# The second sample of attention is loaded during the last tile of the projections, into the projections' own weights buffer

## The reference

```python
q = einsum('bsd,ed->bse', x, Wq)         # 32 heads of 128
k = einsum('bsd,ed->bse', x, Wk); v = ...(Wv)    # 8 heads of 128
q, k = rope(rmsnorm(q)), rope(rmsnorm(k))
kc = k_cache[block_table].reshape(b, 512, 8, 128); vc = v_cache[block_table]...
scores = einsum('bqhd,bkhd->bhqk', q, [kc, k]) * SCALE, masked by cache_seqlens
o = einsum('bhqk,bkhd->bqhd', softmax(scores), [vc, v])
x = x + einsum('bse,de->bsd', o, Wo)
```

## Time and profile before

| | |
|---|---|
| median of 3 runs | 2142.75 us (2140.83 to 2142.89) |
| profiled execution, device time | 2139.18 us |
| span of its trace | 2137.4 us |
| PE busy | 96% of the span |
| granted TensorE clock, mean | 0.99 |
| last matmul of the projections' blocks | starts at 740.4 us |
| first matmul of attention | 753.3 us |

### The profile page before, as it was taken

How to read it: one execution, slowest core, us unless ns; L and a number is a source line. 1 busy time by engine, 2 the same in 40 slices (tenths; PEclk the granted TensorE clock), 3 DMA queues, 4 the chain that set the end, 5 groups by cost and what they waited for, 6 DMA issues and landing times.

```text
span 2137.4 us, 55695 instructions
## 1 busy us (share of the span) xinstructions
PE 2060.5 (96%) x17217; PEld 1346.7 (63%) x17217; DVE 1673.6 (78%) x4284; ACT 1476.5 (69%) x4204; POOL 1102.1 (52%) x1854
## 2 busy tenths in 40 slices
PE   5898999999999878999999999999999999999999
PEld 3444555555555456777777777777777777777775
DVE  7787888887877676778777777777777777777774
ACT  2575777777777766777777777777777777777774
POOL 4464656565666544545445454545454545454542
PEclk9999999999999989999999999999999999999999
DMA  9555787876677589988888888788888888887881
GB/s 352 188 204 168 220 255 225 249 221 210 205 235 246 195 296 280 302 262 250 248 257 249 248 250 259 240 253 249 250 250 248 254 254 246 251 256 246 250 243 55
DMA packets 415961, 513.97 MB, mean 240 GB/s; under 512 B 67251, under 2 KB 313907, under 8 KB 413108
## 3 DMA queue, kind: packets, MB, share of 16 engines
q1 hardware_dynamic: 378292, 375.65, 57.3%
q0 software_dynamic: 37376, 134.76, 19.6%
HBM read 413.77 MB, written 92.54 MB: 237 GB/s over the span
## 4 chain that ended last, share of the span: by engine, by line
PE 60%; SPq 1%; DVE 1%; DMA 1%; issue 1%; ACT 0%; POOL 0%; POOLq 0%; DVEq 0%; ACTq 0%
PE att_scores L1619 15%; PE att_y L1669 15%; PE att_tr L1628 11%; PE att_o L1655 5%; PE att_o L1656 5%; PE att_o L1657 5%; PE att_tr_new L1634 1%; PE att_o L1658 1%; PE att_scores L1620 1%; SPq L126 1%; SPq L120 1%; DMA att_keys<-k_parts 1%; DVE att_prob L1772 0%; DMA att_values<-v_parts,att_idx 0%; DVE att_tpl L1796 0%
## 5 line engine op out<-in xcount | busy, mean ns | idle before, releaser
L1772 DVE CUSTOM_DVE_ANT_0 att_prob<-att_scores,att_mask 128x544 f32<-128x544 f32 x512 | 370.7, 724 | 291.6 <-PE att_scores L1620 238.5
L1698 ACT ACTIVATE att_tph<-att_tr 128x512 f16<-128x512 f32 x512 | 305.9, 597 | 326.2 <-PE att_tr L1628 316.4
L1568 POOL CAST att_parts<-att_norm 128x96 f16<-128x96 f32 x512 | 135.1, 264 | 560.9 <-issue 553.5
L1669 PE MATMUL att_y<-att_wo,att_ot 128*128 128x512 f16 x1536 | 407.6, 379 | 0.0
L1796 DVE TENSOR_TENSOR att_tpl<-att_tr,att_tph 128x512 f16<-128x512 f32 x512 | 349.9, 683 | 0.6 <-ACT att_tph L1698 0.5
L1628 PE MATMUL att_tr<-ident,att_norm 128*128 128x128 f32 x2048 | 325.8, 282 | 0.0
L1225 POOL TENSOR_TENSOR proj_rn<-proj_ra,proj_rb 128x512 f32<-128x512 f32 x128 | 190.3, 1487 | 204.0 <-DVE proj_rb L1334 191.7
L1655 PE MATMUL att_o<-att_tph,att_values 128*128 128x128 f16 x1536 | 284.0, 219 | 2.7 <-ACT att_of L1698 2.3
L1657 PE MATMUL att_o<-att_tph,att_values 128*128 128x128 f16 x1536 | 284.0, 219 | 0.0
L1656 PE MATMUL att_o<-att_tpl,att_values 128*128 128x128 f16 x1536 | 283.9, 219 | 0.0
L1789 DVE TENSOR_SCALAR att_norm<-att_prob,att_col 128x544 f32<-128x544 f32 x512 | 254.2, 497 | 1.0 <-issue 1.0
(11 more groups left out here) (227 smaller groups left out, 5301.6 us busy)
## 6 DMA issues: line engine op xcount, KB each, us to landing
room<-k_parts SPq DMA_DIRECT2D x512, 128.0 KB, 2.7
att_keys<-k_parts SPq DMA_DIRECT2D x512, 128.0 KB
q_parts<-proj_turned SPq DMA_DIRECT2D x128, 256.0 KB, 3.6
v_new_parts<-proj_vp SPq DMA_DIRECT2D x64, 256.0 KB, 3.1
room<-q_parts SPq DMA_DIRECT2D x32, 512.0 KB, 6.8
att_query<-q_parts SPq DMA_DIRECT2D x32, 512.0 KB
w<-in_w_t SPq DMA_DIRECT2D x12, 1024.0 KB, 21.5
room<-in_k_t SPq DMA_DIRECT2D x8, 1024.0 KB, 5.9
```

The lines of the kernel that those rows point to most:

```text
L1669: last = mm(y_ps[:, :], ot[p][:, a, h, :], wo[:, h, w, :], start=(h == 0 and start), stop=(h == HQ - 1 and stop))
L1698: copy = lambda out, in_, **kw: nc.scalar.activation(out, in_, ACT.Copy, **kw)
L1772: v.tensor_tensor_reduce(out=prob[q][:, :], in0=sc[q], in1=mask[bi % 2][:, at:at + LK], scale=1.0, scalar=-3.0e38, op0=ALU.add, op1=ALU.ma ...
```

## The change

`w` becomes a buffer of the whole program and is laid out by chunk first, `[P, WN, KD, 2, WC]`. Its first half (chunks 0 to 2) is used by blocks 0 to 5 alone. When the last tile has made these, the second sample's keys, query, all four parts of its values and its fresh values are loaded there, and the two parts of the first sample's values that were fetched at the start of attention. SP issues the 26 transfers at step 7 of the last tile, POOL its 6 gathers after its sums 6 to 9. In attention sample 1 is not loaded again, 24 of the 32 heads of `wo` lie in the second half of `w`, and its 8 pieces are issued in another order. The weights' loads in mixing keep their number and size, but write two runs of 4 KB in each partition where they wrote one of 8 KB.

```diff
+SAMPLE = 16 * (NPP + 2 + HB + BT)
...
+        w = keep("w", [P, WN, KD, 2, WC], F16)
...
+        half = WN // 2 * KD * 2 * WC
+        columns = w[:, :, :, :, :].rearrange("p c k h m -> p (c k h m)")
+        take = taker(columns[:, 0:half], half)
+        keys1 = take([NPP + 1, HK, 2, PS], F16)
+        query1 = take([HK, 2, P], F16)
+        values1 = [take([HK, 2, HD], F16) for _ in range(LC)]
+        fresh1 = take([HK, HD], BF16)
+        values0 += [take([HK, 2, HD], F16) for _ in range(LC - EV)]
+        wo_here = columns[:, half:2 * half].rearrange("p (h two d) -> p h two d", two=2, d=D)
...
-            w = mid("w", [P, KD, WN, 2, WC], F16)
...
-                sp.dma_start(raw(i), w_t[k * P:(k + 1) * P, c:c + CH]).then_inc(w_in[i // 3], 16)
+                sp.dma_start(raw(i), w_t[k * P:(k + 1) * P, c:c + CH].rearrange("p (n m) -> p n m", m=WC)).then_inc(w_in[i // 3], 16)
...
+        LATER = {6: (2,), 7: (3, 4), 8: (5, 6), 9: (7,)}
...
+            def second_sample():
+
+                sp.wait_ge(early, SAMPLE)
+                sp.wait_ge(blk_done, (NT - 1) * BLK + BLK // 2)
+                load_sample(nc, sp, 1, 0, 1, keys[1], query[1], rscale[1], page0, k_d, kn_d, q_d, rs_d, early)
+                load_fresh(sp, 1, fresh[1], vn_d, early)
...
+                    if t == NT - 1 and n == BLK // 2 + 1:
+                        second_sample()
...
-            sp.wait_ge(early, 16 * (NPP + 2 + HB + BT))
...
+            def later_values(c):
+
+                if c == EV:
+                    pool.wait_ge(early_values, 16 * EV)
+                    pool.wait_ge(blk_done, (NT - 1) * BLK + BLK // 2)
+                g.indirect_dma_start(out=values[c // LC][c % LC][:, :, :].rearrange("p h two d -> p (h two d)"),
...
                     add(t, n)
+                    if t == NT - 1 and n >= BLK // 2:
+                        for c in LATER[n]:
+                            later_values(c)
...
-        WO_BEHIND = {1: (0,), 2: (1, 2), 3: (3,), 4: (4,), 5: (5,), 6: (6,), 7: (7,)}
+        WO_BEHIND = {0: (0, 1, 2), 2: (3, 4), 3: (5,), 4: (6,), 5: (7,)}
...
-                    if past or bi:
+                    if past or bi > 1:
                         load(t, bi)
...
-                    if c >= 0 and (bi < BT or not (isinstance(t, int) and t == NT - 1)):
+                    if c >= 0 and (bi < BT or t < NT - 1) and t * BT + bi > 1:
                         gather(t * BT + bi, bi % 2, c)
```

More of the change, by code:

```diff
@@ L198, in conditional_residual @@
         fresh0 = take([HK, HD], BF16)
-        page0 = take([NPP], I32)[0:1]
-        first = (keys0, query0, values0, fresh0, rscale0, page0)
+        page0 = take([2 * NPP], I32)[0:1]
+        half = WN // 2 * KD * 2 * WC
[7 more added lines that the diff above has]
+        wo_here = columns[:, half:2 * half].rearrange("p (h two d) -> p h two d", two=2, d=D)
+        samples = ((keys0, keys1), (query0, query1), (values0, values1), (fresh0, fresh1), rscale, page0)
+        early, early_values = (whole.enter_context(nc.semaphore(s)) for s in ("early_samples", "early_values"))
         ab = ExitStack()
@@ L788, in _, with projections @@
                 x_step(i)
-def projections(nc, ident, ident16, mag, pow2, up, down, oscale, iota, cs, vw, cos, sin, wa, wb, w, x3, col, xh, xl, xt0, first, taker, v_idx, pages, wo_t, k_t, v_rows,
+def projections(nc, ident, ident16, mag, pow2, up, down, oscale, iota, cs, vw, cos, sin, wa, wb, w, x3, col, xh, xl, xt0, samples, early, early_values, taker, v_idx, pages, wo_t, k_t, v_rows,
                 x3_d, q_d, rs_d, kn_d, vn_d, k_d, v_d, wo_d):
@@ L832, in projections @@
         XHIGH = 5
-        keys0, query0, values0, fresh0, rscale0, page0 = first
+        LATER = {6: (2,), 7: (3, 4), 8: (5, 6), 9: (7,)}
+        keys, query, values, fresh, rscale, page0 = samples
         NWO = HQ
@@ L1092, in body @@
                     for k in range(KD):
-                        wh, wl = (w[:, k, chunk, h, at:at + D] for h in range(2))
+                        wh, wl = (w[:, chunk, k, h, at:at + D] for h in range(2))
                         mm(out, xt[p][:, k, 0, :], wh, start=(k == 0), stop=False)
@@ L1394, in _, with attention @@
                 heads_low(NT - 1, QB + j)
-def attention(nc, ident, ident16, oscale, iota, v_idx, lens_f, first, k_d, v_d, kn_d, vn_d, q_d, rs_d, wo_d, x3_d,
+def attention(nc, ident, ident16, oscale, iota, v_idx, lens_f, samples, early, early_values, wo_here, k_d, v_d, kn_d, vn_d, q_d, rs_d, wo_d, x3_d,
               out_v, pages):
@@ L1412, in sem @@
             return ctx.enter_context(nc.semaphore("att_" + name))
-        keys0, query0, values0, fresh0, rscale0, page0 = first
-        rscale = [rscale0, sb("rscale1", [P, HK], F32)]
+        keys, query, values, fresh, rscale, page0 = samples
         norm = [sb(f"norm{i}", [P, LK], F32) for i in range(2)]
-        wo = sb("wo", [P, HQ, 2, D], F16)
-        keys = [keys0, sb("keys1", [P, NPP + 1, HK, 2, PS], F16)]
-        values = [[sb(f"values{p}_{c}", [P, HK, 2, HD], F16) if p or c >= EV else values0[c] for c in range(LC)]
-                  for p in range(2)]
+        WOH = 4
+        HERE = wo_here.shape[1]
+        wo_rest = sb("wo", [P, HQ - HERE, 2, D], F16)
         page_row = sb("page_row", [1, B * NPP], I32)
-        fresh = [fresh0, sb("fresh1", [P, HK, HD], BF16)]
-        query = [query0, sb("query1", [P, HK, 2, P], F16)]
         idx = [sb(f"idx{i}", [P, LC], U32) for i in range(2)]
@@ L1474, in quad_views, with wo_of @@
             return src, [ot[p][:, a, heads, bi * S:(bi + 1) * S] for a in range(2)]
[L1477 to L1478 removed]
+        WO_BEHIND = {0: (0, 1, 2), 2: (3, 4), 3: (5,), 4: (6,), 5: (7,)}
+        def wo_of(first, last):
+            return wo_here[:, first:last] if last <= HERE else wo_rest[:, first - HERE:last - HERE]
         block = ctx.enter_context(nc.Block())
@@ L1668, in project @@
                 for a, w, start, stop in ((0, 0, True, False), (0, 1, False, False), (1, 0, False, True)):
-                    last = mm(y_ps[:, :], ot[p][:, a, h, :], wo[:, h, w, :], start=(h == 0 and start),
+                    last = mm(y_ps[:, :], ot[p][:, a, h, :], wo_of(h, h + 1)[:, 0, w, :], start=(h == 0 and start),
                               stop=(h == HQ - 1 and stop))
```

66 lines of the change are left out of this document (33 added, 33 removed).

## The result

The changed kernel is slower: 2155.38 us median of 6 runs (2151.6 to 2159.03) against 2142.82 of the kernel before beside it, a ratio of 1.0062 (95% interval 1.0046 to 1.0078). Its profiled execution took 2156.13 us, with a span of 2154.4 us, 17.0 more than the span of before; that one lay 3.6 us under its median, so the trace shows the loss larger than the runs do (17.0 against 12.6 us).

What follows compares the result with a forecast made beforehand. PE bounds the kernel, busy 2060.5 of 2137.4 us. The terms +9.4 - 0.4 - 1.6 - 0.4 + 0.2 = +7.2 us on the median 2142.75 gave 2150.0 us; range 2139 to 2158, the forecast's own bounds 2146 to 2154.

Steps and rivals of the forecast that it cites:

- The block on SP ahead of the stores of heads 3 to 9: Last tile: sample 1's 26 loads delay block 3's store, so ACT's copy of block 7 and attention start 9.4 us late.
- The upper end of 16.8: Upper bound in us of attention's delay, with row scales issuing 5.2 longer and the store landing 2.2 later.
- The gathers cost nothing: POOL's six gathers between sums 6 to 9 of the last tile hold nobody up: 0 us.
- Attention, -0.4 - 1.6 - 0.4: Gains in us forecast inside attention: for sample 0, for samples 2 and 3, and from sample 4 on.
- The first -0.4: Attention, sample 0: four gathers leave its steps 4 to 7, so one of POOL's four holds of PE goes.
- the -1.6: Attention, samples 2 and 3: `wo` goes out 1.6 us earlier, shortening two waits; bounds 0 and -8.6.
- the signs: What would show the forecast; in attention, waits for values in sample 2 and keys in sample 3, together 5 us or more.
- The argument for little gain: Samples 2 and 3: `wo` pieces again stand behind them, and sample 1's removed transfers did not reach that far.
- The rival of the full gain: All waits of samples 2, 3 and later go, -10.3 us, with a delay of 8.0: 2140.7 us; chance 0.2.
- Blocked longer: Rival: row scales held by gathers, block 3's store lands late, up to +16.8 us for +9.4: 2157 us; chance 0.15.
- Faster: Rival: SP finishes the 26 loads in time, ACT is not held, delay 0 to 1 us: 2133 to 2141 us; chance 0.15.
- Weights in runs of 4 KB, +0.2: Mixing: weights' loads written in two runs of 4 KB cost 0.2 us more; bounds 0 and +2.

Runs made afterwards that it cites:

- e3: Changed kernel with sample 1's four gathers back in attention, SP's 26 transfers still at step 7 of the last tile; ratio 1.0028 to the kernel before.
- e11: Changed kernel with SP's 26 transfers at step 11 of the last tile, behind the stores of heads 3 to 6; ratio 1.0055 to the kernel before.
- e5: Changed kernel with six pieces of `wo` issued at the start of attention, none behind samples 2 and 3; 2144.26 us, ratio 1.0006 to the kernel before.
- e2: Changed kernel with SP's load of sample 1 back in attention and the old `wo` order, gathers still early; ratio 1.0006 to the kernel before.
- e1: Changed kernel with only its new buffers kept, every transfer issued where the kernel before issues it; ratio 1.0007 to the kernel before.
- e4: Changed kernel with SP's transfers for sample 1 spread over gaps of the last tile, some left to attention; 2149.33 us, ratio 1.0027 to the kernel before.
- e12: Changed kernel with only 8 pages early on SP, 18 transfers first in attention, then four `wo` pieces; 2135.71 us, ratio 0.9972 to the kernel before.

## Why the prediction was right, and where it was off

*The block on SP ahead of the stores of heads 3 to 9:* right in place and in kind (block 7's copy held by a DMA `q_parts`; e3 and e11), too small in size. The term was +9.4 us and measured 14.4 at the copy, 14.75 at the first score, in this one trace; e5, with the same instructions there, has 12.0 at the first score from the projections' start. The difference by its parts: the transfers began at 731.86 and not at 730.2 (1.7), for the values' stores took 2.61 us to issue in place of 2.10 and the whole tile ran 1.1 us later; issuing took 16.8 us and not 15.1 (1.7), of it 1.0 in the new keys and the query and 0.8 in the row scales (3.13 against 2.37); block 3's store went out 0.57 us behind the block in place of 0.5 (0.1); and it landed 6.1 us after its issue (749.23 to 755.35), not 4.5 (1.6). 1.7 + 1.7 + 0.1 + 1.6 = 5.1, the difference of 5.0 up to rounding. The upper end of 16.8 was worked out from the right two terms, the row scales and the landing, and the value between the ends was taken too near to the quiet ones. (That the issuing measured 16.8 us too is chance.)

*The gathers cost nothing:* within noise alone (e2), wrong beside the block, where they add 1.3 to 3.9 us at the first score (e3 against e5 and the changed kernel) by the landing of that store, and more over the runs.

*Attention, -0.4 - 1.6 - 0.4:* it measured +2.3 in these two traces, which is no gain; kernels that put the same load on DMA there (e1, e3, e4) lie at 1384.8 to 1386.8, so a loss is not shown either. The first -0.4 is not there: POOL's parts hold PE four times for 1.6 us as before. Of the -1.6, the two pieces of `wo` do go out 1.1 us sooner after the load of sample 2 begins (15.8 us for 16.9), from the row scales (1.97 for 3.24), while the 16 pages take 10.19 us to issue in both; and it bought nothing, since the waits sum to 10.9 us and not to less than 9.5. The keys were late in sample 4 and not in sample 3, as the signs had it. The argument for little gain, that the changed table again puts two pieces behind sample 2 and one behind sample 3, is borne out: moving these pieces alone gives 13.8 us (12 over the runs, e5). Its other half, that sample 1's transfers "did not reach that far", holds for this change, since the waits stayed when these transfers left. But it is not the whole: the row of 0.72 DMA share at 784 us showed that the backlog had drained, not that its time was useless. Filled with pieces, that time brings attention to 1372.6 us, 11.5 less than before (1384.1).

*The rival of the full gain* (all waits gone, -10.3 us) named an amount that is there, 11.5 us from 1384.1 to 1372.6; it takes the edit of e5. *Blocked longer* is what came: 2155.4 us lies in its band (2154 to 2159), which had a chance of 0.15, and outside the forecast's own (2146 to 2154), which had 0.5. Its two reasons both measured longer, the row scales by 0.8 us and the landing by 1.6, about half of the 5.0. That its 2157 us comes so near is in part luck: it had 16.8 us of delay, where 14.75 came, and kept a gain of 2.4 us in attention, where none came. *Faster* needed SP through its transfers in 7 us; it took 16.8.

*Weights in runs of 4 KB, +0.2:* not resolved. DVE's wait for them was 4.0 us in place of the 3.7, and mixing's length varies by 4 us among kernels that are alike there.

## What to carry to other kernels

A transfer moved into an earlier stage costs what it stands in front of in its queue: count every issue, and see which stores behind it must have landed before a buffer or the stage is free. Put such issues into the queue's gaps, in small groups, and leave the rest where it was (e12 with 8 pages early and four pieces first is faster than e5 with all 26 transfers in one block and six, 0.9972 against 1.0006). And bandwidth that is freed is only worth something if a transfer that now collides is moved into it: look for the stretch in which DMA falls to zero.

## What the runs showed of the hardware

The same store of 256 KB took 3.1 us to land in the quiet stretch, 4.5 beside one sample's load, and a median of 6.3 us in the changed kernel from 745 to 753 us:

```profile
q_parts<-proj_turned SPq DMA_DIRECT2D x4, 256.0 KB, 6.3
```

At that time the engines moved 360 GB/s in the mean, all 16 busy nearly throughout, for pages of 1 KB rows and gathers of 4 KB rows. From 735 to 756 us three kinds of company can be told apart: e2 (six gathers, no load on SP), e3 (SP's block and two gathers), e4 (SP's transfers spread among the stores, six gathers), in this order:

```profile
q_parts<-proj_turned SPq DMA_DIRECT2D x3, 256.0 KB, 5.5
q_parts<-proj_turned SPq DMA_DIRECT2D x4, 256.0 KB, 2.9
q_parts<-proj_turned SPq DMA_DIRECT2D x3, 256.0 KB, 9.9
```

In e3 the stores go out behind the block, and its two gathers had been issued by 740 us: they land as in the quiet stretch. Beside six gathers alone the landing takes nearly twice that (e2), and beside gathers and pages three times (e4).

The small transfers took longer to issue when the queue was loaded, the pages hardly: the four row scales took 1.97 us in the quiet stretch at 789 us of the changed kernel, 3.13 in its block, 4.93 in that of e11 and up to 7.40 before, while the 16 pages took 8.7 to 10.2 us throughout.

PE's clock was at its lower level for 3 to 7 us around each long wait for data in attention (about 819 to 823 and 853 to 861 us in the changed kernel), and at that level it made 25 matmuls in 4 us of busy time for 40 at the upper one. By that a wait costs more than its own length.
